# ScalarE copies a chunk's high part directly behind its square, on a three-stream block of Trainium2

## The chip, the core and the metric

The kernel runs on one core of one Trainium2 chip. The metric is device time in microseconds (us), smaller is better. Engines are named as in the profile: PE (TensorE), PEld (its weight loads), DVE (VectorE), ACT (ScalarE), POOL (GpSimd), SP (the queue that starts most transfers).

## What is computed

x is 32 sequences of 256 tokens of 128 numbers. The block is a "macaron": half a mixture of experts, attention, half a mixture of experts, each behind a layer norm.

```python
x = x + 0.5 * ffn(layernorm(x)); x = x + attention(layernorm(x)); x = x + 0.5 * ffn(layernorm(x))
# ffn: 8 experts, widths 4 x 128 and 4 x 256 (1536 columns in all), the best two of each token
topw, sel = top_k(sigmoid(xf @ router_w.T), 2); topw = topw / topw.sum(-1)
h = square(relu(einsum('td,edw->tew', xf, W1e)))
out = einsum('td,te->td', einsum('tew,ewd->ted', h, W2e), combine)
# attention: 16 heads of 8, rotary, linear: features elu + 1, k_feat^T v per sequence, then divided
```

## The kernel before, in words

Tokens go in 16 groups of 512. A group passes three streams: f1 (first expert layer), at (attention), f2 (second expert layer). One iteration t of a pipeline, written out on every engine, works on f1's group t+1, on attention's groups t-1 and t-2 and on f2's group t-4, and on the preparations of later groups. Iterations run from t = -3 to 21; f1 lives in t = -1 to 14, f2 in t = 4 to 19. From t = 4 to 13 both run at full density. Each engine's order is the order of the calls in its `iteration`; nothing but semaphores couples the engines.

Each expert layer is cut into NC = 12 chunks of 128 hidden columns. The functions of a chunk, in order:

- PE `up` (L532 to L534): three products, since a float32 product is made of a high and a low part of each operand, into one of two banks.
- DVE `weighted` (L1129): relu times the root of the expert's weight, into `hid`, a ring of six slots. Called "gate" below.
- ACT `squares`: the square L781, in place in `hid`, and the copy L792, which rounds to `h_hi`.
- POOL `remainders` (L942): `h_lo = hid - h_hi`; it frees the slot of `hid`.
- PE `down` (L555 to L557): three products with the second weights, nine places behind the chunk's `up`.

An iteration has 24 places, and three places make a quarter: PE's `quarter(t, j)` and ACT's `squares(t, j)` take quarter j. With both streams alive f1's chunks lie on places 0 to 11 and f2's on 12 to 23: three chunks a quarter. A stream that is alone (`alone`) has its chunks on every second place. `squares` waits for the gate before each square, for the square before its copy, and before the first copy of a quarter also for older `down` products, which free `h_hi`.

Around the quarters ACT does other work: `evacuate_x` copies transposed tokens from the bank `tp` to `xT` (L749), `copy_yT` (L808), `norm` (L736), `exp_logits` (L758, L762), `copy_attnT` (L834), and `rows_of_weights` (L770), which copies the transposed expert weights out of the same bank `tp` to `g_row`. PE's transposes into `tp` (L494) wait in `tp_free` for the last reader of the bank, L770 among them. Of ACT's order, quarters 0 and 1 end with L770 of f2; then come xT of the attention, yT, quarters 2 and 3, L834 and xT of f2 (which waits until POOL's L928 has made the attention's x_lo, since `xT` is one buffer).

DVE's `high_part` casts `xT` to `x_hi` (L1047); f2's stands behind place 12 of the gates, and behind it `spread_roots` (L1107, `pick`) of f1, then the gate of place 13. POOL's order has f1's `root_of_weights` (L934), the attention's `low_part` (L928) and so on between its remainders.

In `squares` the local `lag` is 1 where f2 has more groups to come, and 0 in the last iterations: with 1 a copy stands behind the square of the next chunk of its quarter.

Of the kernel before, what the change touches and what calls it, by code (L numbers as in the profile page):

```python
# [30 lines left out]
ACT = mybir.ActivationFunctionType  # L31
# [6 lines left out]
TG = BG * RT  # L38
# [8 lines left out]
NC = WTOT // P  # L47
CQ = NC // TG
STAGE = NC // 2
# [18 lines left out]
class Step:  # L68
# [14 lines left out]
    @property  # L83
    def last(self):
        return self.c + self.a * (self.trips - 1)

    @property
    def value(self):
        return self.i * self.a + self.c


def first(v):
    return v.c if isinstance(v, Step) else v
# [10 lines left out]
def due(v):  # L104

    assert (first(v) > 0) == (last(v) > 0)
    return first(v) > 0


def live(n):  # L110

    return first(n) >= 0 and last(n) < NG
# [7 lines left out]
def done(n):  # L120

    if last(n) <= 0:
        return 0
    if first(n) >= NG:
        return NG
    assert first(n) >= 0 and last(n) <= NG
    return n
# [41 lines left out]
def build(nc, x_in, wqkv, wout, router, w1, w2, const, out, rows):  # L169
    ctx = ExitStack()  # L170
    with ctx:
        def sb(name, shape, dt=F32):
            return ctx.enter_context(nc.sbuf_tensor(name, shape, dt))
# [20 lines left out]
        hid = sb("hid", [P, STAGE, NTOK])  # L194
        h_hi = sb("h_hi", [P, NC, NTOK], F32R)
# [88 lines left out]
        def per(name, keys):  # L284
            return {s: sem(f"s_{name}_{s}") for s in keys}
# [30 lines left out]
        s_z = per("z", FFN)  # L316
        s_sq = per("sq", FFN)
        s_hhi = per("hhi", FFN)
        s_hlo = per("hlo", FFN)
        s_p2 = per("p2", FFN)  # L320
# [7 lines left out]
        other = {"f1": "f2", "f2": "f1"}  # L328
        off = {"f1": 0, "f2": SHIFT}

        def turns(s, t):


            return done(t + 1 + (1 if s == "f2" else 0) - off[other[s]])

        def alone(s, t):


            return not live(t + 1 - SHIFT) if s == "f1" else not live(t + 2)
# [21 lines left out]
        def chunks(t, place, behind=0):  # L361


            out = []
            for s, start in (("f1", 0), ("f2", NC)):
                for back in range(2):
                    k = place + PLACES * back - start - behind
                    step = 2 if alone(s, t - back) else 1
                    n = t - back + 1 - off[s]
                    if live(n) and k % step == 0 and 0 <= k // step < NC:  # L370
                        out.append((s, n, k // step, back))
            return out
# [345 lines left out]
        def _(act):  # L718
            fn = nc.scalar.activation
# [52 lines left out]
            def squares(t, j):  # L772

                todo = [k for place in range(CQ * j, CQ * (j + 1)) for k in chunks(t, place)]
                lag = 0 if alone("f2", t if 2 * j >= TG else t - 1) else 1
                for k in range(len(todo) + lag):
                    if k < len(todo):
                        s, n, c, ago = todo[k]
                        h = hid[:, c % STAGE, :]
                        act.wait_ge(s_z[s], value(n * NC + c + 1))  # L780
                        fn(h, h, ACT.Square).then_inc(s_sq[s], 1)  # L781
                    if k >= lag:
                        s, n, c, ago = todo[k - lag]
                        if c % CQ == 0 or k == lag:
                            m = turns(s, t - ago) * TG + (c // CQ + 1 - TG)
                            if due(m):
                                act.wait_ge(s_p2[other[s]], value(m))
                            m = n * TG + (c // CQ + 1 - TG)
                            if due(m):
                                act.wait_ge(s_p2[s], value(m))  # L790
                        act.wait_ge(s_sq[s], value(n * NC + c + 1))
                        fn(h_hi[:, c, :], hid[:, c % STAGE, :], ACT.Copy).then_inc(s_hhi[s], 1)  # L792

            def copy_yT(s, n, t):
                if not live(n):
# [43 lines left out]
            def iteration(t, par):  # L839
                n1, n2, n2_last = t + 1, t + 1 - SHIFT, t - SHIFT  # L840
                evacuate_x("f1", t + 2, t, 0)
                squares(t - 1, 7)
                norm("at", t - 1)
                exp_logits("f1", t + 2)
                squares(t, 0)
                norm("f2", t + 2 - SHIFT)
                squares(t, 1)
                rows_of_weights("f2", n2)
                if alone("f1", t):
# [511 lines left out]
```

## Time and profile before

| | us |
|---|---|
| median of three runs | 774.03 |
| the three | 774.02, 774.03, 774.63 |
| the profiled execution | 772.65 |
| its span, first to last instruction | 770.8 |

The span is what the profile shows; 1.85 us of the profiled execution lie around it. TensorE's granted clock was 0.997 on average, that is its higher level throughout. Page rows give busy time, instruction count and, behind a bar, the idle time before a group of instructions with what ended most of it. Timeline rows give start, duration, engine, line, operation and tiles, a count where several were merged, and in brackets the idle time before with its releaser. Instructions of one engine overlap a little, so a start can lie before the end of the one before.

### The profile page before, as it was taken

The page shows a single profiled execution, that of the slowest core. Times are in us where ns is not written, and L with a number is a line of the kernel's source. Part 1 is how long each engine was busy: PE and PEld are TensorE (multiplying, and loading weights), DVE is VectorE, ACT ScalarE, POOL GpSimd, SP SyncE. Part 2 cuts the span into 40 slices and gives each one's busy share as a digit, 9 for nine tenths or more (in the row PEclk, how much of TensorE's full clock was granted, in tenths as well). Part 3 has the DMA queues.
Part 4 walks back from the last instruction along what each step waited for, and adds up shares of the span by engine and source line. Part 5 has one row for each costly group of instructions (what it writes and reads, how often), then busy time and mean ns, then how long its engine had stood idle before and what let it go on. Part 6 is the DMA issues. An engine that isn't in the chain of part 4 may idle for free.

```text
span 770.8 us, 13299 instructions
## 1 busy us (share of the span) xinstructions
PE 724.6 (94%) x3736; PEld 592.4 (77%) x3736; DVE 584.3 (76%) x1834; ACT 602.0 (78%) x1221; POOL 685.4 (89%) x663
## 2 busy tenths in 40 slices
PE   6899888789999999999999999999999999899888
PEld 6677676668888878888888888888887877777666
DVE  4767887887778797978778797978778587785554
ACT  4688767587888889788888889788878776767876
POOL 3899887879999999999999999999999877686986
PEclk9999999999999999999999999999999999999999
DMA  5553303212233332213333331323333302123331
GB/s 185 192 194 111 111 3 109 95 44 87 107 111 124 111 125 107 77 63 101 123 111 124 111 125 48 114 76 110 124 111 124 112 14 111 36 90 124 122 110 43
DMA packets 31176, 79.38 MB, mean 103 GB/s; under 512 B 3328, under 2 KB 14464, under 8 KB 31104
## 3 DMA queue, kind: packets, MB, share of 16 engines
q1 hardware_dynamic: 30816, 78.47, 29.9%
q8 instruction: 30, 0.49, 0.3%
q14 instruction: 42, 0.34, 0.1%
q10 hardware_dynamic: 288, 0.07, 0.1%
HBM read 73.81 MB, written 4.72 MB: 102 GB/s over the span
## 4 chain that ended last, share of the span: by engine, by line
PE 29%; DVE 27%; POOL 16%; issue 13%; ACT 11%; DMA 3%; DVEq 1%; POOLq 0%; ACTq 0%; SPq 0%
POOL h_lo L942 9%; DVE hid L1129 7%; PE bank L532 4%; PE bank L534 3%; PE bank L533 3%; PE bank L555 3%; POOL root_f L934 3%; PE bank L557 3%; PE bank L556 3%; ACT h_hi L792 3%; ACT hid L781 3%; DVE pick_f L1107 2%; DMA g_all_f<-rows_f 2%; PE bank L651 2%; PE bank L639 2%
## 5 line engine op out<-in xcount | busy, mean ns | idle before, releaser
L942 POOL TENSOR_TENSOR h_lo<-hid,h_hi 128x512 fp32r<-128x512 f32 x383 | 492.1, 1310 | 47.1 <-ACT h_hi L792 46.3
L1129 DVE SCALAR_TENSOR_TENSOR hid<-bank,g_all_f 128x512 f32<-128x512 f32 x384 | 262.6, 684 | 126.0 <-PE bank L534 87.9
L781 ACT ACTIVATE hid<-hid 128x512 f32<-128x512 f32 x384 | 229.6, 621 | 26.7 <-DVE hid L1129 26.1
L792 ACT ACTIVATE h_hi<-hid 128x512 fp32r<-128x512 f32 x384 | 229.0, 622 | 9.0 <-ACT hid L781 0.8
L532 PE MATMUL bank<-x_hi_f,w_hi 128*128 128x512 f32 x384 | 163.9, 427 | 13.5 <-DVE hid L1129 13.4
L555 PE MATMUL bank<-h_hi,w_hi 128*128 128x512 f32 x384 | 153.5, 400 | 4.7 <-POOL h_lo L942 4.5
L557 PE MATMUL bank<-h_hi,w_lo 128*128 128x512 f32 x384 | 152.1, 396 | 0.0
L534 PE MATMUL bank<-x_hi_f,w_lo 128*128 128x512 f32 x384 | 151.6, 395 | 0.0
L533 PE MATMUL bank<-x_lo_f,w_hi 128*128 128x512 f32 x384 | 151.5, 395 | 0.0
L556 PE MATMUL bank<-h_lo,w_hi 128*128 128x512 f32 x384 | 151.3, 394 | 0.0
L532 PEld LDWEIGHTS bank<-x_hi_f,w_hi 128*128 128x128 f32 x384 | 72.8, 190 | 37.4 <-DVE hid L1129 20.7
L555 PEld LDWEIGHTS bank<-h_hi,w_hi 128*128 128x128 f32 x384 | 72.2, 188 | 24.4 <-POOL h_lo L942 8.9
L534 PEld LDWEIGHTS bank<-x_hi_f,w_lo 128*128 128x128 f32 x384 | 72.5, 189 | 17.4
L557 PEld LDWEIGHTS bank<-h_hi,w_lo 128*128 128x128 f32 x384 | 72.2, 188 | 16.7
L556 PEld LDWEIGHTS bank<-h_lo,w_hi 128*128 128x128 f32 x384 | 72.2, 188 | 15.3
L533 PEld LDWEIGHTS bank<-x_lo_f,w_hi 128*128 128x128 f32 x384 | 73.1, 190 | 10.9
L934 POOL TENSOR_TENSOR root_f<-cwt_f,c_half 128x8 f32<-128x8 f32 x32 | 54.1, 1690 | 3.8 <-DVE cwt_f L1089 3.7
L736 ACT ACTIVATE xn_f<-x_sb,nbias_f,rstd_f 128x128 f32<-128x128 f32 x120 | 49.1, 481 | 8.0 <-POOL nbias_f L910 8.0
L928 POOL TENSOR_TENSOR x_lo_f<-xT,x_hi_f 128x512 fp32r<-128x512 f32 x32 | 41.5, 1298 | 11.3 <-DVE x_hi_f L1047 11.3
L749 ACT ACTIVATE xT<-bank 128x512 f32<-128x512 f32 x48 | 28.4, 592 | 27.8 <-PE bank L494 20.9
L758 ACT ACTIVATE ex_f<-bank 128x32 f32<-128x32 f32 x32 | 6.3, 198 | 43.4 <-PE bank L513 43.4
L1047 DVE CAST x_hi_f<-xT 128x512 fp32r<-128x512 f32 x32 | 20.6, 645 | 25.5 <-ACT xT L749 25.5
(118 smaller groups left out, 1050.4 us busy)
## 6 DMA issues: line engine op xcount, KB each, us to landing
g_all_f<-rows_f SPq DMA_DIRECT2D x128, 512.0 KB, 5.5
x_sb<-in_x SPq DMA_DIRECT2D x16, 256.0 KB, 3.4
out_x<-x_sb SPq DMA_DIRECT2D x15, 256.0 KB, 7.0
g_all_f<-in_w SPq DMA_DIRECT2D x2, 768.0 KB, 6.8
con<-in_const SPq DMA_DIRECT2D x1, 584.0 KB, 6.3
rows_f<-g_row_f SPq DMA_DIRECT2D x32, 16.0 KB, 1.4
out_x<-x_sb SPq DMA_DIRECT2D x2, 128.0 KB, 1.8
g_all_f<-in_wqkv SPq DMA_DIRECT2D x1, 192.0 KB, 6.5
```

The costliest lines, as they stand in the source:

```text
L532: mm(o, w1_hi[:, w], x_hi[s][u][:], start=True, stop=False)
L533: mm(o, w1_hi[:, w], x_lo[s][u][:], start=False, stop=False)
L534: mm(o, w1_lo[:, w], x_hi[s][u][:], start=False, stop=True).then_inc(s_p1[s], 1)
L555: mm(o, w2_hi[:, c, :], h_hi[:, c, :], start=(c == 0), stop=False)
L556: mm(o, w2_hi[:, c, :], h_lo[:, c, :], start=False, stop=False)
L557: i = mm(o, w2_lo[:, c, :], h_hi[:, c, :], start=False, stop=(c == NC - 1))
L736: i = fn(xn[s][:, k, :], tile, ACT.Identity, bias=shift[:, first + k:first + k + 1], scale=scale[:, first + k:first + k + 1])
L781: fn(h, h, ACT.Square).then_inc(s_sq[s], 1)
L792: fn(h_hi[:, c, :], hid[:, c % STAGE, :], ACT.Copy).then_inc(s_hhi[s], 1)
L934: gp.tensor_tensor(root[s][:], cwt[s][:], c_half[:], ALU.pow).then_inc(s_root[s], 1)
L942: gp.tensor_tensor(h_lo[:, c, :], hid[:, c % STAGE, :], h_hi[:, c, :].bitcast(F32), ALU.subtract).then_inc(s_hlo[s], 1)
L1129: v.scalar_tensor_tensor(hid[:, c % STAGE, :], hp[c % 2][:], 0.0, g_all[s][:, EXPERT[c], :], ALU.max, ALU.mult).then_inc(s_z[s], 1)
```

## The change

`squares` loses its `lag`. Every copy L792 now stands directly behind the square of its own chunk, in all iterations; waits and instructions are the same. Before, the order was such only from quarter 2 of t = 14 on.

```diff
                 todo = [k for place in range(CQ * j, CQ * (j + 1)) for k in chunks(t, place)]
-                lag = 0 if alone("f2", t if 2 * j >= TG else t - 1) else 1
-                for k in range(len(todo) + lag):
-                    if k < len(todo):
-                        s, n, c, ago = todo[k]
-                        h = hid[:, c % STAGE, :]
-                        act.wait_ge(s_z[s], value(n * NC + c + 1))
-                        fn(h, h, ACT.Square).then_inc(s_sq[s], 1)
-                    if k >= lag:
-                        s, n, c, ago = todo[k - lag]
-                        if c % CQ == 0 or k == lag:
...
+                for k, (s, n, c, ago) in enumerate(todo):
+                    h = hid[:, c % STAGE, :]
+                    act.wait_ge(s_z[s], value(n * NC + c + 1))
+                    fn(h, h, ACT.Square).then_inc(s_sq[s], 1)
+                    if c % CQ == 0 or k == 0:
+                        m = turns(s, t - ago) * TG + (c // CQ + 1 - TG)
+                        if due(m):
+                            act.wait_ge(s_p2[other[s]], value(m))
+                        m = n * TG + (c // CQ + 1 - TG)
+                        if due(m):
+                            act.wait_ge(s_p2[s], value(m))
+                    act.wait_ge(s_sq[s], value(n * NC + c + 1))
+                    fn(h_hi[:, c, :], hid[:, c % STAGE, :], ACT.Copy).then_inc(s_hhi[s], 1)
```

ACT's row in a two-stream iteration, from quarter 3 to the attention copy, f2's xT and f1's norm, before:

```order
L781 ACTIVATE hid<-hid 128x512 x2
L792 ACTIVATE h_hi<-hid 128x512
L781 ACTIVATE hid<-hid 128x512
L792 ACTIVATE h_hi<-hid 128x512 x2
L834 ACTIVATE attn<-bank 128x512
L749 ACTIVATE xT<-bank 128x512
L736 ACTIVATE xn_f<-x_sb,nbias_f,rstd_f 128x128 x4
```

and the same place now (the lines behind the function moved up by five, so L778 is the square, L787 the copy, L829 the attention copy):

```order
L778 ACTIVATE hid<-hid 128x512
L787 ACTIVATE h_hi<-hid 128x512
L778 ACTIVATE hid<-hid 128x512
L787 ACTIVATE h_hi<-hid 128x512
L778 ACTIVATE hid<-hid 128x512
L787 ACTIVATE h_hi<-hid 128x512
L829 ACTIVATE attn<-bank 128x512
L749 ACTIVATE xT<-bank 128x512
L736 ACTIVATE xn_f<-x_sb,nbias_f,rstd_f 128x128 x4
```

The first copy moved ahead of the second square and the second copy ahead of the third; what follows the quarter is in its old place.

ACT's row at quarter 1, with f2's norm ahead of it and the row of weights, xT of the attention and yT behind it, before:

```order
L736 ACTIVATE xn_f<-x_sb,nbias_f,rstd_f 128x128 x4
L781 ACTIVATE hid<-hid 128x512 x2
L792 ACTIVATE h_hi<-hid 128x512
L781 ACTIVATE hid<-hid 128x512
L792 ACTIVATE h_hi<-hid 128x512 x2
L770 ACTIVATE g_row_f<-bank,c_cut 32x128
L749 ACTIVATE xT<-bank 128x512
```

and now:

```order
L736 ACTIVATE xn_f<-x_sb,nbias_f,rstd_f 128x128 x4
L778 ACTIVATE hid<-hid 128x512
L787 ACTIVATE h_hi<-hid 128x512
L778 ACTIVATE hid<-hid 128x512
L787 ACTIVATE h_hi<-hid 128x512
L778 ACTIVATE hid<-hid 128x512
L787 ACTIVATE h_hi<-hid 128x512
L770 ACTIVATE g_row_f<-bank,c_cut 32x128
L749 ACTIVATE xT<-bank 128x512
```

The same exchange; L770 still stands behind the quarter's last copy. PE's, DVE's, POOL's and SP's orders are as before.

## Rows read from the trace of the kernel before

**Rows 1.** The page, busy time of each engine.
```profile
PE 724.6 (94%) x3736; PEld 592.4 (77%) x3736; DVE 584.3 (76%) x1834; ACT 602.0 (78%) x1221; POOL 685.4 (89%) x663
```

**Rows 2.** Busy time by stretch: stretch, its length, busy us of each engine, clock, DMA.
```profile
156.00:592.00 436.00, 430.35 (x2234) 358.24 (x2234) 351.94 (x1134) 361.12 (x754) 423.85 (x402) 1.00 0.31 103
...
300.00:343.57 43.57, 43.25 (x227) 36.11 (x226) 35.37 (x115) 36.42 (x76) 43.03 (x42) 1.00 0.31 104
```

**Rows 3.** The page, the costliest group of instructions.
```profile
L942 POOL TENSOR_TENSOR h_lo<-hid,h_hi 128x512 fp32r<-128x512 f32 x383 | 492.1, 1310 | 47.1 <-ACT h_hi L792 46.3
```

**Rows 4.** Timeline of ACT in the iteration from 300 us, quarters 2 and 3.
```profile
301.83 1.15 ACT L781 ACTIVATE hid<-hid 128x512 f32<-128x512 f32 x2
302.87 0.63 ACT L792 ACTIVATE h_hi<-hid 128x512 fp32r<-128x512 f32 x1
...
308.08 0.58 ACT L834 ACTIVATE attn<-bank 128x512 f32<-128x512 f32 x1
309.33 0.60 ACT L749 ACTIVATE xT<-bank 128x512 f32<-128x512 f32 x1 [0.67 <-POOL x_lo_at L928]
```

**Rows 5.** Timeline of POOL, the same place.
```profile
302.22 1.29 POOL L942 TENSOR_TENSOR h_lo<-hid,h_hi 128x512 fp32r<-128x512 f32 x1
...
303.58 1.30 POOL L942 TENSOR_TENSOR h_lo<-hid,h_hi 128x512 fp32r<-128x512 f32 x1
...
309.12 1.29 POOL L942 TENSOR_TENSOR h_lo<-hid,h_hi 128x512 fp32r<-128x512 f32 x1
...
310.38 1.46 POOL L942 TENSOR_TENSOR h_lo<-hid,h_hi 128x512 fp32r<-128x512 f32 x1
```

**Rows 6.** Timeline of DVE, the same iteration.
```profile
303.63 1.52 DVE L1047 CAST x_hi_at<-xT 128x512 fp32r<-128x512 f32 x1
...
309.96 0.73 DVE L1047 CAST x_hi_f<-xT 128x512 fp32r<-128x512 f32 x1 [2.11 <-ACT xT L749]
310.62 1.30 DVE L1107 TENSOR_TENSOR pick_f<-chosen_f,root_f 128x64 f32<-128x64 f32 x1
311.84 0.68 DVE L1129 SCALAR_TENSOR_TENSOR hid<-bank,g_all_f 128x512 f32<-128x512 f32 x1
...
330.91 0.41 DVE L1047 CAST x_hi_f<-xT 128x512 fp32r<-128x512 f32 x1
331.24 0.21 DVE L1107 TENSOR_TENSOR pick_f<-chosen_f,root_f 128x64 f32<-128x64 f32 x1
```

**Rows 7.** Timeline of ACT where the order is already the new one (t = 14).
```profile
605.86 0.63 ACT L781 ACTIVATE hid<-hid 128x512 f32<-128x512 f32 x1
606.60 0.63 ACT L792 ACTIVATE h_hi<-hid 128x512 fp32r<-128x512 f32 x1
607.14 0.62 ACT L781 ACTIVATE hid<-hid 128x512 f32<-128x512 f32 x1
607.79 0.63 ACT L792 ACTIVATE h_hi<-hid 128x512 fp32r<-128x512 f32 x1
...
609.51 0.61 ACT L781 ACTIVATE hid<-hid 128x512 f32<-128x512 f32 x1
610.52 0.63 ACT L792 ACTIVATE h_hi<-hid 128x512 fp32r<-128x512 f32 x1 [0.39 <-ACT hid L781]
```

**Rows 8.** Timeline, the row of weights on ACT and PE's transposes behind it.
```profile
342.82 0.34 ACT L770 ACTIVATE g_row_f<-bank,c_cut 32x128 f32<-32x128 f32 x1
...
343.79 0.60 PE L494 MATMUL bank<-con,xn_at 128*128 128x128 f32 x4
```

**Rows 9.** The lonely first stream: timelines of ACT and PE, and POOL's waits from 20 to 160 us.
```profile
66.70 0.62 ACT L781 ACTIVATE hid<-hid 128x512 f32<-128x512 f32 x1
...
68.75 1.14 ACT L792 ACTIVATE h_hi<-hid 128x512 fp32r<-128x512 f32 x2
...
137.33 1.16 PE L670 MATMUL bank<-wout_sb,attn 128*128 128x128 f32 x8 [0.23 <-ACT attn L834]
...
POOL h_lo L942 <- ACT h_hi L792: 12.0, 12, 1.9
```

More of the change, by code:

```diff
@@ L774, in squares @@
                 todo = [k for place in range(CQ * j, CQ * (j + 1)) for k in chunks(t, place)]
-                lag = 0 if alone("f2", t if 2 * j >= TG else t - 1) else 1
-                for k in range(len(todo) + lag):
-                    if k < len(todo):
-                        s, n, c, ago = todo[k]
-                        h = hid[:, c % STAGE, :]
-                        act.wait_ge(s_z[s], value(n * NC + c + 1))
-                        fn(h, h, ACT.Square).then_inc(s_sq[s], 1)
-                    if k >= lag:
-                        s, n, c, ago = todo[k - lag]
-                        if c % CQ == 0 or k == lag:
[L785 to L792, printed above, removed]
+                for k, (s, n, c, ago) in enumerate(todo):
[11 more added lines that the diff above has]
+                    fn(h_hi[:, c, :], hid[:, c % STAGE, :], ACT.Copy).then_inc(s_hhi[s], 1)
             def copy_yT(s, n, t):
```

## The prediction

> **What bounds the kernel now.** I read the profile from the outside in. The page first: a span of 770.8 us in which PE is busy 94%, GpSimd (POOL) 89% and ScalarE (ACT) 78% [rows 1]. That is an average over stages, so the table by stage comes next [rows 2]. From 156 to 592 us both mixture-of-experts streams run at full density: ten iterations, PE busy 430.35 of 436.00 us. The reader is to see one of them, from 300.00 to 343.57 us: PE busy 43.25 and POOL 43.03 of its 43.57 us, ACT 36.42. Two engines are full at once, so anything that makes either wait lengthens the iteration; ACT has room in the sum, but not at every place. Before 156 us the first stream is alone, and looser.
>
> POOL's bulk is 383 remainders of 1310 ns, one for each chunk, each behind one of ScalarE's copies L792 [rows 3]. Then the timelines, engine by engine, of that one iteration. On ACT, a quarter with three chunks issues its six instructions 0.52 us apart although each lasts 0.62; two quarters take 308.08 - 301.83 = 6.25 us [rows 4]. The first copy starts at 302.87 and ends at 303.50, and POOL's remainder starts at 303.58: POOL, whose remainder before ended at 303.51, waits for this copy by a hair [rows 5]. I call the start of this copy zero. From zero, POOL works without a pause; one of its operations ends and the next begins at +7.51 (310.38). On DVE, the cast L1047 of x_hi for the second stream is asked for at +7.09 (309.96, after 2.11 us of waiting for ACT's xT); pick L1107 follows, and the 14th gate of the iteration starts at +8.97 (311.84) [rows 6]. From there DVE's timeline shows no idle time until the attention's features, where it waits for ScalarE's exponential, and what it makes feeds PE, which is full until the transposes L494 that release ACT for the next zero. So there is a circle: zero, ACT's two quarters, attention copy, xT, cast, pick, DVE, PE, transposes, zero. It and POOL's own work are almost equally long, and both are 43.57.
>
> **The cost of the change, part by part.** No instruction is added or removed: 384 squares and 384 copies stay. The only order that moves is ACT's, in quarters of two or three chunks, up to the first two quarters of the iteration that begins at 592 us; from the third quarter of that one on the kernel has the new order already, and its rows there give the price.
>
> Part 1, the copy behind its own square. In the order already new (605.86 on) a quarter takes 609.51 - 605.86 = 3.65 us: square to copy 0.74 and then 0.65, copy to square 0.54 [rows 7]. The old quarter takes 6.25 / 2 = 3.12. So a three-chunk quarter costs ACT +0.53, and two neighbouring quarters +1.05. The first copy of a quarter, however, starts 0.74 behind its square and not 302.87 - 301.83 = 1.04: -0.30. One copy there started 1.01 behind its square (609.51 to 610.52); bound for that: nothing or +0.27 more in a quarter. I take nothing, since the others show 0.65 to 0.74.
>
> Part 2, zero comes 0.30 earlier for POOL and for everything counted from it: -0.30 an iteration on the circle.
>
> Part 3, the attention copy and xT behind two quarters. Today the attention copy starts at +5.21. New: 7.30 - 0.74 = +6.56. xT follows 0.48 behind (duration 0.58 less 0.10 of overlap) and takes 0.60, and DVE starts 0.03 behind its end: +7.67 instead of +7.09. Today's 0.67 us in which ACT waits there for POOL's x_lo [rows 4] swallows the rest. What is late next: the cast. The rows show what a DVE cast does beside a POOL remainder. L1047 lasts 0.41 us at 330.91, but 1.52 at 303.63, where it came 0.05 behind the start of a remainder, and it ended at 305.15, when that remainder had ended (304.88) [rows 5, 6]. pick lasts 0.21 at 331.24 and 1.30 at 310.62, ending at 311.92, just behind the end of a remainder at 311.84 (310.38 + 1.46). So these two run on DVE only between two POOL operations. Today the cast comes at +7.09, before the boundary at +7.51, and pick gets the boundary after that. At +7.67 the cast misses it by 0.16 us: it gets the next, one remainder later (310.38 - 309.12 = 1.26), and pick and the gate behind it move by as much: **+1.26 an iteration**. DVE and PE have no room behind it, so this reaches the next zero.
>
> The Trainium skill ("SBUF — State Buffer", Who interferes with whom) states that a VectorE operation in a 2-port mode, or with two SBUF inputs against a GpSimd operation that reads SBUF, blocks fully for the whole instruction, and casts and tensor_tensor are among them; the trace agrees [rows 5, 6]. By that rule the term is 1.26. If the long durations were no such lock and the cast merely came late, the term would be the delay itself, 0.58.
>
> Part 4, the row of weights. Two quarters before L770 make it 1.05 later: its end, 343.16 today, goes to 344.21. PE's transposes L494 (start 343.79) write the bank that L770 reads, and wait for it [rows 8]. The slack is 0.63 us, so at least 1.05 - 0.63 = +0.42; at most all 1.05, should PE's queue need after the release what it has today. DVE starts 0.03 behind the xT that it waits for [rows 4, 6], which speaks for the low end; with a little for PE's queue I take +0.60.
>
> An iteration: 1.26 + 0.60 - 0.30 = +1.56; ten of them, +15.6 us. POOL will then wait about 1.6 us for the copy at zero.
>
> Part 5, the lonely first stream (five iterations). Here a copy often waits for the next chunk's square, which waits for DVE: square 66.70, its copy 68.75 [rows 9]; new, 66.70 + 0.74 = 67.44, a gain of 1.3. All of POOL's waits for copies are 12.0 us, in 12 places, and only some lie on the path, in the first two iterations: I take -1.5 of bounds 0 and -2.6 (two of 1.3). In the later ones PE's output product waits for the attention copy [rows 9], which comes behind three chunks and so later by up to 0.53: for two such iterations +0.8. Together -0.7; if a window as in part 3 is missed there once, +0.6.
>
> **Sum:** +15.6 - 0.7 = +14.9 on a span of 770.8. The profiled run took 772.65, the median of three is 774.03; the difference is carried over unchanged: **788.9 us**. This case with its own bounds (part 4 from 0.42 to 1.05, part 5 from -2.6 to +1.4 around it) is 785 to 794.
>
> **The rivals.** (a) The window is kept: the cast still gets in before +7.51, since it misses by 0.16 us only and POOL's first operations could start later by as much. Then an iteration changes by 0.60 - 0.30 = +0.3: +3 - 0.7, 776.3. For it speaks the smallness of the miss; against it that POOL starts 0.08 behind the copy's end every time and that 0.05 was enough to lose at 303.63. (b) The delay is passed on with no lock: 0.58 + 0.3 = 0.88 an iteration, 782.1. Against it stand the picks of 1.30 us (one row shown for ten alike, [rows 6]). (c) Faster: the circle has hidden room (at the cast 2.11 us of idle DVE, at L494 0.63 of slack), POOL alone sets the period, and the copies that come early help. Then ten iterations give POOL's hair back, some 0.07 each (303.58 against 303.51), and the lonely stage up to 2.6: 771. It decides from there whether ACT's +1.05 in two quarters fits into its waits: it would if the 0.67 us before xT were 1.05. Against it: 0.67 is less. (d) Worse: L494 late by all of 1.05, the odd copy of 1.01 (+0.27) in each pair of quarters, and one more DVE operation meeting a remainder: 1.26 + 1.05 + 0.27 - 0.30 + about 0.4 = 2.7 an iteration, 800. (e) That the edit does nothing to the order is excluded: ACT's order shows the copies moved.
>
> **Chances.** Forecast 0.58, (a) 0.14, (b) 0.10, (c) 0.11, (d) 0.07. The range leaves out (c) and (d) for the most part: 775 to 794. About 0.2% is what a measurement of this kernel can tell from no change, 1.5 us. Faster by more than that: (c), 0.11. Within: the lower part of (a), 0.07. Slower: 0.82.
>
> **What would show it.** In the iterations between 156 and 592 us: period about 45.1 instead of 43.57; ACT's quarter of three 3.65; cast L1047 of the second stream over 1 us long and ending some 9.1 behind zero; the gate behind pick at about +10.2; L494 right behind L770; POOL idle 1.6 us before the remainder at zero, with PE's busy time unchanged in sum. A cast of 0.7 us or less there, or a POOL without idle time, would show part 3 wrong; L494 more than 0.5 us behind L770's end would show part 4 mis-sized. If the time is within 3 us of 774, the circle was not the bound.

## The result, and the profile after

| | before | after |
|---|---|---|
| median of the runs, us | 774.02 | 793.97 |
| lowest and highest | 773.54 to 774.63 | 792.7 to 794.29 |
| the profiled execution | 772.65 | 794.29 |
| its span | 770.8 | 792.5 |

The changed kernel is slower: ratio 1.0255, interval 1.024 to 1.0271. The forecast was 788.9 with a range of 775 to 794. The sign and the mechanism held; the size was 5.1 us too small, and the result stands at the very end of the range.

The page of the changed kernel, busy time of each engine, the chain that ended last by engine, and the groups of the remainder and of DVE's cast:

```profile
PE 731.4 (92%) x3736; PEld 593.0 (75%) x3736; DVE 597.6 (75%) x1834; ACT 629.9 (79%) x1221; POOL 683.6 (86%) x663
...
PE 38%; DVE 23%; ACT 19%; issue 12%; DMA 3%; POOL 3%; DVEq 1%; ACTq 0%; POOLq 0%; SPq 0%
...
L937 POOL TENSOR_TENSOR h_lo<-hid,h_hi 128x512 fp32r<-128x512 f32 x383 | 490.8, 1306 | 67.4 <-ACT h_hi L787 66.9
...
L1042 DVE CAST x_hi_f<-xT 128x512 fp32r<-128x512 f32 x32 | 28.0, 876 | 27.5 <-ACT xT L749 27.5
```

The same groups of before:

```profile
PE 29%; DVE 27%; POOL 16%; issue 13%; ACT 11%; DMA 3%; DVEq 1%; POOLq 0%; ACTq 0%; SPq 0%
...
L1047 DVE CAST x_hi_f<-xT 128x512 fp32r<-128x512 f32 x32 | 20.6, 645 | 25.5 <-ACT xT L749 25.5
```

POOL's remainders cost what they did (490.8 against 492.1 us, [rows 3]), but the time in which POOL waits for a copy rose from 47.1 to 67.4 us. POOL's own work fell from 16% to 3% of the chain that ended last; that share alone proves little, since pad_104 below, as fast as the kernel before, shows 3% as well. And a DVE cast, an instruction that nobody touched, became 231 ns longer on average.

**Where the time is.** Zero is, as in the prediction, the start of the first copy of quarter 2. Three zeros of after, with the square ahead of each, on ACT's timeline:

```profile
173.90 0.61 ACT L778 ACTIVATE hid<-hid 128x512 f32<-128x512 f32 x1
174.60 0.63 ACT L787 ACTIVATE h_hi<-hid 128x512 fp32r<-128x512 f32 x1
...
355.55 0.63 ACT L778 ACTIVATE hid<-hid 128x512 f32<-128x512 f32 x1
356.29 0.63 ACT L787 ACTIVATE h_hi<-hid 128x512 fp32r<-128x512 f32 x1
...
627.22 0.63 ACT L778 ACTIVATE hid<-hid 128x512 f32<-128x512 f32 x1
627.97 0.63 ACT L787 ACTIVATE h_hi<-hid 128x512 fp32r<-128x512 f32 x1
```

and the first of before, and two neighbouring ones (its last, at 606.60, stands in [rows 7]):

```profile
172.22 0.61 ACT L792 ACTIVATE h_hi<-hid 128x512 fp32r<-128x512 f32 x1
...
346.44 0.63 ACT L792 ACTIVATE h_hi<-hid 128x512 fp32r<-128x512 f32 x1
...
390.00 0.63 ACT L792 ACTIVATE h_hi<-hid 128x512 fp32r<-128x512 f32 x1
```

From the first to the last zero are ten periods: 453.37 us after, 434.38 before, so +18.99, that is +1.90 a period. Ahead of the first zero there is +2.38, behind the last 164.53 against 164.20, +0.33. Together 21.7 of 21.7 us of span. The ten iterations hold the loss. The medians differ by less than these two executions, 19.95 us; with 18.99 in the ten periods, some 1 us of them is left for all other stages.

**One period.** The period that begins at 356.29, DVE's timeline from the second stream's cast to the gate behind pick, then from cw_f on:

```profile
363.94 1.43 DVE L1042 CAST x_hi_f<-xT 128x512 fp32r<-128x512 f32 x1 [2.38 <-ACT xT L749]
365.30 1.30 DVE L1102 TENSOR_TENSOR pick_f<-chosen_f,root_f 128x64 f32<-128x64 f32 x1
366.52 0.68 DVE L1124 SCALAR_TENSOR_TENSOR hid<-bank,g_all_f 128x512 f32<-128x512 f32 x1
...
376.36 0.63 DVE L1080 TENSOR_TENSOR cw_f<-best_f,rtot_f 128x8 f32<-128x8 f32 x1
...
383.95 0.69 DVE L1202 SCALAR_TENSOR_TENSOR kf<-kb,ka 128x512 f32<-128x512 f32 x1 [0.79 <-ACT kb L813]
...
385.16 0.69 DVE L1124 SCALAR_TENSOR_TENSOR hid<-bank,g_all_f 128x512 f32<-128x512 f32 x1
385.76 0.47 DVE L1042 CAST x_hi_f<-xT 128x512 fp32r<-128x512 f32 x1
```

The cast now comes at +7.65, lasts 1.43 instead of 0.73 us [rows 6], and the gate behind pick starts at +10.23 instead of +8.97. It took the boundary that the prediction named: on POOL's timeline a block of three remainders begins at 362.55 (+6.26), so its second begins near +7.5 and its third near +8.8; the cast came behind the former and ended at 365.37, 0.3 us behind the latter.

```profile
357.00 1.31 POOL L937 TENSOR_TENSOR h_lo<-hid,h_hi 128x512 fp32r<-128x512 f32 x1 [1.81 <-ACT h_hi L787]
...
362.55 3.96 POOL L937 TENSOR_TENSOR h_lo<-hid,h_hi 128x512 fp32r<-128x512 f32 x3
```

cw_f, with two inputs in SBUF, is new in the story. In the same place of before it lasted 0.16 us, and kf lasted 0.91:

```profile
365.32 0.16 DVE L1085 TENSOR_TENSOR cw_f<-best_f,rtot_f 128x8 f32<-128x8 f32 x1
...
372.45 0.91 DVE L1207 SCALAR_TENSOR_TENSOR kf<-kb,ka 128x512 f32<-128x512 f32 x1 [0.80 <-ACT kb L818]
```

The end of the period, ACT's row of weights and PE's transposes behind it, up to the zero at 401.73:

```profile
398.80 0.34 ACT L770 ACTIVATE g_row_f<-bank,c_cut 32x128 f32<-32x128 f32 x1
...
399.35 0.63 PE L494 MATMUL bank<-con,xn_at 128*128 128x128 f32 x4 [0.54 <-issue]
...
401.73 0.63 ACT L787 ACTIVATE h_hi<-hid 128x512 fp32r<-128x512 f32 x1
```

The transposes start 0.21 us behind the end of L770 (399.14). Before there were 0.63 us between the two [rows 8].

For the whole sum I take the first stream's cast as a marker: before 330.91, which is 28.04 behind its zero [rows 4, 6]; after 385.76, +29.47. From the marker to L494: before 343.79 - 330.91 = 12.88 [rows 6, 8], after 13.59. From L494 to the next zero: before 346.44 - 343.79 = 2.65, after 2.38. So the period grew by 1.43 + 0.71 - 0.27 = 1.87 (45.44 against 43.57).

### The profile page after: what moved, and what is told of

Its sections match the earlier page's. It is cut to its first block, busy times and chain, and to the rows that moved or that the text cites. A ratio compares the mean times of both kernels' runs of the same rounds, so it can differ in the third digit from the quotient of the medians.

```text
span 792.5 us, 13299 instructions
## 1 busy us (share of the span) xinstructions
PE 731.4 (92%) x3736; PEld 593.0 (75%) x3736; DVE 597.6 (75%) x1834; ACT 629.9 (79%) x1221; POOL 683.6 (86%) x663
## 4 chain that ended last, share of the span: by engine, by line
PE 38%; DVE 23%; ACT 19%; issue 12%; DMA 3%; POOL 3%; DVEq 1%; ACTq 0%; POOLq 0%; SPq 0%
ACT h_hi L787 7%; ACT hid L778 6%; DVE hid L1124 6%; PE bank L532 5%; PE bank L534 5%; PE bank L533 5%; PE bank L555 5%; PE bank L557 4%; PE bank L556 4%; DMA g_all_f<-rows_f 2%; PE bank L651 2%; PE bank L639 2%; PE bank L513 2%; DVE pick_f L1102 2%; ACT kb L813 1%
## 5 line engine op out<-in xcount | busy, mean ns | idle before, releaser
L937 POOL TENSOR_TENSOR h_lo<-hid,h_hi 128x512 fp32r<-128x512 f32 x383 | 490.8, 1306 | 67.4 <-ACT h_hi L787 66.9
L787 ACT ACTIVATE h_hi<-hid 128x512 fp32r<-128x512 f32 x384 | 242.9, 633 | 26.1 <-ACT hid L778 1.5
L778 ACT ACTIVATE hid<-hid 128x512 f32<-128x512 f32 x384 | 237.4, 618 | 22.8 <-DVE hid L1124 22.4
L555 PEld LDWEIGHTS bank<-h_hi,w_hi 128*128 128x128 f32 x384 | 72.6, 189 | 21.7 <-POOL h_lo L937 6.0
L556 PEld LDWEIGHTS bank<-h_lo,w_hi 128*128 128x128 f32 x384 | 72.5, 189 | 15.6
L1042 DVE CAST x_hi_f<-xT 128x512 fp32r<-128x512 f32 x32 | 28.0, 876 | 27.5 <-ACT xT L749 27.5
L513 PEld LDWEIGHTS bank<-router_sb,xT 128*128 128x128 f32 x256 | 33.1, 196 | 3.0 <-ACT xT L749 1.6
```

What stands on the lines that cost most here:

```text
L555: mm(o, w2_hi[:, c, :], h_hi[:, c, :], start=(c == 0), stop=False)
L556: mm(o, w2_hi[:, c, :], h_lo[:, c, :], start=False, stop=False)
L937: gp.tensor_tensor(h_lo[:, c, :], hid[:, c % STAGE, :], h_hi[:, c, :].bitcast(F32), ALU.subtract).then_inc(s_hlo[s], 1)
```

## The experiments

The theory is that of the prediction: the two-quarter delay makes the cast miss a boundary of POOL's work (part 3), the row of weights holds back L494 (part 4), and nothing else matters. Rivals: the delay is passed on as it is, without a lock; the 2.4 us ahead of the first zero are the lonely stage's price; the period would be set by something else. All ratios are against the kernel before, run on the same chip in the same session (its medians there were 774.0 to 774.6), with a 95% interval in brackets. Positions in the table are relative to zero, read from the timelines, for the period that begins nearest to 350 us; the length of the cast in us stands in brackets.

| kernel | cast asked at (length) | gate behind pick | marker | marker to L494 | L494 to zero | period |
|---|---|---|---|---|---|---|
| before | +7.10 (0.74) | +8.98 | +28.04 | 12.88 | 2.65 | 43.57 |
| after | +7.65 (1.43) | +10.22 | +29.47 | 13.59 | 2.38 | 45.44 |
| q23_old | +7.09 (0.74) | +8.98 | +28.02 | 13.48 | 2.68 | 44.18 |
| q01_old | +7.65 (1.42) | +10.21 | +29.47 | 12.88 | 2.35 | 44.70 |
| q03_old | +7.10 (0.74) | +8.98 | +28.04 | 12.87 | 2.65 | 43.56 |
| pad_104 | +7.35 (0.47) | +8.98 | +28.04 | 12.88 | 2.65 | 43.57 |
| pad_135 | +7.65 (1.42) | +10.20 | +29.42 | 12.87 | 2.65 | 44.94 |
| xT_first | +7.15 (0.70) | +8.99 | +29.20 | 13.59 | 2.38 | 45.17 |
| gate_first | +7.64 (1.43) | gate first | +29.48 | 13.59 | 2.38 | 45.45 |
| gate_cw | +7.64 (1.42) | gate first | +29.15 | 13.59 | 2.39 | 45.13 |

### Parts of the change alone: q23_old, q01_old, q03_old

Each is the kernel before with one condition in `squares`. q23_old keeps the old order in quarters 2 and 3 of the ten full iterations:

```diff
-                lag = 0 if alone("f2", t if 2 * j >= TG else t - 1) else 1
+                lag = 1 if 4 <= t <= 13 and j in (2, 3) else 0
```

> The changed kernel, but in the ten iterations with both streams (t = 4 to 13) quarters 2 and 3 keep the old order; nothing else is undone. Window theory: the cast L1047 of the second stream comes again at +7.1 behind the first copy of quarter 2, lasts 0.7, the gate behind pick is back at +9.0, and a period falls from 45.46 to about 44.2 (less 1.25; the 0.27 that the first copy gains goes too, and the late row of weights, +0.72, stays). Total about 794.0 - 9.8 = 784. Rival, plain lateness without a lock (0.57 an iteration): about 791. Rival, ACT as a whole too full: half of the loss back, 784 as well, but then the cast would not jump from 1.4 to 0.7 us.

Measured: 780.82 us, ratio 1.0088 (1.0063 to 1.0114). The period is 44.18, the cast and the gate are where they were before, and what grew is marker to L494, by exactly the 0.60 of part 4. The time is 3 us under the expected 784, which had counted the old order in quarters 2 and 3 as worth 1.25 - 0.27 a period; it is worth 1.26 (45.44 - 44.18), because the 0.18 between gate and marker and 0.11 at L494 go with it. On q23_old's timelines the marker, ACT's row of weights, PE's transposes and the next zero:

```profile
381.02 0.41 DVE L1047 CAST x_hi_f<-xT 128x512 fp32r<-128x512 f32 x1
...
393.95 0.34 ACT L770 ACTIVATE g_row_f<-bank,c_cut 32x128 f32<-32x128 f32 x1
...
394.50 0.63 PE L494 MATMUL bank<-con,xn_at 128*128 128x128 f32 x4 [0.44 <-issue]
...
397.18 0.63 ACT L792 ACTIVATE h_hi<-hid 128x512 fp32r<-128x512 f32 x1
```

L770 ends 13.27 behind the marker, 1.02 later than before (343.16 - 330.91 = 12.25); the slack of 0.63 swallows part of that, and 0.21 for the release are added: 1.02 - 0.63 + 0.21 = 0.60.

q01_old is the mirror image, old order in quarters 0 and 1:

```diff
-                lag = 0 if alone("f2", t if 2 * j >= TG else t - 1) else 1
+                lag = 1 if 4 <= t <= 14 and j in (0, 1) else 0
```

> The changed kernel, but in the two-stream iterations quarters 0 and 1 keep the old order. Theory: the row of weights L770 is in time again, PE's transposes L494 are not held, a period is 45.46 - 0.72 = 44.7 and the total about 794.0 - 7 = 787. The cast still misses its window (1.4 us, gate at +10.2). If the late row of weights cost nothing, the total stays at 794.

Measured: 785.39 us, ratio 1.0162 (1.0133 to 1.0191); period 44.70. Marker to L494 is that of before, the cast has missed its boundary, and L494 to zero is 0.30 shorter, which is part 2. So +1.43 - 0.30 = +1.13. The two halves give 0.61 + 1.13 = 1.74 of the 1.87; the rest is in marker to L494, 13.59 with both against 13.48.

q03_old has the old order in quarters 0 to 3 and the new one in all others:

```diff
-                lag = 0 if alone("f2", t if 2 * j >= TG else t - 1) else 1
+                lag = 1 if 4 <= t <= 14 and j in (0, 1) or 4 <= t <= 13 and j in (2, 3) else 0
```

> Quarters 0 to 3 of the two-stream iterations in the old order, quarters 4 to 7 and everything else in the new. Theory: both causes are gone, period 43.6 to 43.8 (the 0.19 us between the gate behind pick and the last gate may stay, since quarters 4 to 7 are behind it), total 776.5 to 778.5 with the 2.4 us that the lonely stage lost. If the cost came from ACT's load in sum, half of 19 us would stay: 784.

Measured: 773.16 us, ratio 0.9994 (0.9976 to 1.0012), under the expected 776.5 to 778.5: neither 0.19 a period nor 2.4 us of the lonely stage stayed. Four of eight quarters take the new order for nothing: the whole price hangs on the four in front of L834 and of L770.

### The cliff alone: pad_104 and pad_135

The kernel before, ACT's order untouched, with spare copies ahead of the attention copy in the ten full iterations. They read the constants and write a buffer that nobody reads. pad_104 has the first two, pad_135 also the third, with 256 columns:

```diff
+                if 4 <= t <= 13:
+                    fn(pads[0][:, 0:512], con[:, 0:512], ACT.Copy)
+                    fn(pads[1][:, 0:512], con[:, 0:512], ACT.Copy)
+                    fn(pads[2][:, 0:256], con[:, 0:256], ACT.Copy)
```

> The kernel before, order untouched, with two spare copies of 128x512 on ACT ahead of the attention copy in the ten two-stream iterations; their output is used by nobody. They make the attention copy 1.04 us later. Window theory: xT waited 0.67 us anyway, so the cast comes at +7.36, before the boundary at +7.51: the window is kept, gate at +9.0, total 774 to 776. Plain lateness: the cast comes 0.27 us later, and the circle with it: 776.7. Load theory (ACT's extra work is what costs, as much as in the change): over 780.

> As pad_104, with a third spare copy of 128x256, 0.31 us more: the attention copy is 1.35 late, the cast comes at +7.67, behind the boundary. Window theory: the cast lasts 1.4 us, the gate stands at +10.2, a period is 44.8 and the total 774 + 12.5 = 786.5, a jump of about 12 us for 0.31 us of work. Plain lateness: 0.58 an iteration, 780, only 3 above pad_104.

Measured: pad_104 774.5 us, ratio 0.9997 (0.9973 to 1.0021); pad_135 787.29 us, ratio 1.017 (1.0136 to 1.0205). DVE's timeline of pad_104 (zero at 348.03):

```profile
355.38 0.47 DVE L1051 CAST x_hi_f<-xT 128x512 fp32r<-128x512 f32 x1 [2.37 <-ACT xT L750]
355.77 1.30 DVE L1111 TENSOR_TENSOR pick_f<-chosen_f,root_f 128x64 f32<-128x64 f32 x1
357.00 0.68 DVE L1133 SCALAR_TENSOR_TENSOR hid<-bank,g_all_f 128x512 f32<-128x512 f32 x1
```

and of pad_135 (zero at 351.74):

```profile
359.39 1.42 DVE L1052 CAST x_hi_f<-xT 128x512 fp32r<-128x512 f32 x1 [2.67 <-ACT xT L750]
360.73 1.29 DVE L1112 TENSOR_TENSOR pick_f<-chosen_f,root_f 128x64 f32<-128x64 f32 x1
361.94 0.68 DVE L1134 SCALAR_TENSOR_TENSOR hid<-bank,g_all_f 128x512 f32<-128x512 f32 x1
```

The first 1.04 us of added ScalarE work an iteration cost nothing that the times show: the cast comes 0.25 later, lasts 0.27 less and ends at the same place. That is as much ScalarE work as the change adds in two quarters, so ScalarE's load as such is not the price. The next 0.31 us cost 12.8 us in all, 1.4 a period. That is a step, not a slope, and rival (b), the delay passed on, falls with it: pad_104 would have cost its 0.25 a period, 2.5 us.

The first of pad_104's ten periods shows the same step inside one run. There POOL's boundary lay earlier, at +7.30 (zero at 172.39), and the cast, asked for at +7.33, had just missed it; DVE's cast and POOL's remainder:

```profile
179.72 1.54 DVE L1051 CAST x_hi_f<-xT 128x512 fp32r<-128x512 f32 x1 [2.92 <-ACT xT L750]
...
179.69 1.30 POOL L946 TENSOR_TENSOR h_lo<-hid,h_hi 128x512 fp32r<-128x512 f32 x1
```

That period took 44.76 us against 43.30 for the first of the kernel before. The nine others took what they did before.

### The lonely stage: lone_new and late_new

lone_new is the kernel before with the new order for t < 4, late_new the changed kernel with the old order for t < 4 (its condition is `lag = 1 if t < 4 else 0`).

```diff
-                lag = 0 if alone("f2", t if 2 * j >= TG else t - 1) else 1
+                lag = 0 if t < 4 or alone("f2", t if 2 * j >= TG else t - 1) else 1
```

> The kernel before with the new order in the lonely iterations of the first stream alone (t up to 3). Theory: the loss of 2.4 us before the first two-stream iteration comes from here alone: 776.4. The prediction's view of the stage: 773.3 (less 0.7).

> The changed kernel with the order of before in the lonely stage (t < 4), the new order from t = 4 on. All agree that the period between two zeros is 45.45 us, as in the changed kernel. If the 2.4 us by which the changed kernel's profiled execution came later to the first full iteration were caused by the order there, this run is 2 us faster than the changed kernel: 791.5. If the new order in the lonely stage is worth about 2 us, as the run with the new order there alone says (-0.25%), this run is slower than the changed kernel, 795 to 796. If neither, 794.

Measured: lone_new 771.47 us, ratio 0.9975 (0.9956 to 0.9994), while late_new took 793.62, ratio 1.0236 (1.0211 to 1.026), not different from the 793.97 of the changed kernel. The first says that the new order gains there, the second that it does nothing; neither says that it costs 2.4 us. before_gate and lone_gate (below) differ by this order alone and took 773.42 and 773.37, which again says nothing. The first zero in the profiled executions came at 170.7 to 173.6 in the five kernels with the old order in that stage, and at 170.1 to 176.5 in the nine with the new one, q23_old the latest and q01_old the earliest of all, although the two have the same program up to t = 4. So the +2.38 is of the size of what one execution differs from another, and the lonely stage's share stays open, between -2 and +2 us.

What such a difference consists of can be read in the changed kernel. DVE's sum of the keys (two inputs in SBUF) in the lonely stage:

```profile
119.18 1.66 DVE L1197 SCALAR_TENSOR_TENSOR ka<-ka,kb 128x512 f32<-128x512 f32 x1
...
123.43 1.51 DVE L1042 CAST x_hi_f<-xT 128x512 fp32r<-128x512 f32 x1
```

The same sum took 0.69 us in the profile of before. It met a remainder there, as the cast did in the full iterations.

### Can the window be bought back: xT_first and gate_first

If a missed boundary is most of the price, other orders should return it. xT_first is the changed kernel with xT of the second stream ahead of the attention copy on ACT:

```diff
-                copy_attnT(t - 2)
...
+                copy_attnT(t - 2)
```

> The changed kernel with one pair of ACT's calls exchanged: xT of the second stream ahead of the attention copy. Window theory: xT starts at +6.55 and the cast at +7.2, before the boundary at +7.51; the cast lasts 0.7, the gate is back at +9.0, the period 44.2, total 794.0 - 12.5 = 781.5, with the new order untouched. If PE's output product then waits for the later attention copy, some of it comes back. Rival (the two quarters' added time costs wherever it lies): 792 to 794.

Measured: 793.48 us, ratio 1.0237 (1.0208 to 1.0266). The expectation missed by 12 us, though its mechanism came true: the cast got its boundary again (+7.15, 0.70 long) and the gate behind pick was back at +8.99. But PE did not move with zero. Against zero its output product L670 starts at +7.76, where it was +7.48 in the kernel before, because zero, the copy close behind its square, is itself some 0.3 earlier. It is not the later attention copy that holds it: in the changed kernel, where that copy is 0.47 earlier, L670 starts at +7.77, and in both PE has no idle time before it (in xT_first its weight load waited 0.18 us for the copy, without moving the product). With the cast in time, PE is what comes last: DVE waits 0.24 us for it ahead of the gate at +11.24 (+10.95 before), so 0.28 a period is lost there, and at +22.18 DVE's comparison for the experts misses a boundary (+21.93). PE's product in xT_first and in the changed kernel, then DVE's timeline of xT_first, cast and gate, and this comparison:

```profile
361.06 1.06 PE L670 MATMUL bank<-wout_sb,attn 128*128 128x128 f32 x8
...
364.07 1.05 PE L670 MATMUL bank<-wout_sb,attn 128*128 128x128 f32 x8
```


```profile
360.46 0.70 DVE L1042 CAST x_hi_f<-xT 128x512 fp32r<-128x512 f32 x1 [1.90 <-ACT xT L749]
...
362.30 0.68 DVE L1124 SCALAR_TENSOR_TENSOR hid<-bank,g_all_f 128x512 f32<-128x512 f32 x1
...
375.49 1.12 DVE L1092 TENSOR_TENSOR chosen_f<-which_f,con 128x64 f32<-128x64 uint32 x1
```

It lasted 1.12 instead of 0.19 us. The marker came at +29.20, only 0.27 earlier than in the changed kernel. Even that does not show in the total: the ten periods took 450.55 us, 2.8 less, but what lies behind the last zero took 169.1 instead of 164.5. The exchange stands in all iterations, and 2.8 us of it are there in the stage of the second stream alone (a copy 87.1 us behind the last zero in the changed kernel comes at 89.9 here); no run tests the exchange there by itself.

gate_first is the changed kernel with the gate of place 13 ahead of cast and pick on DVE, where DVE is idle:

```diff
+                weighted(t, 13)
                 high_part("f2", n2, p2)
                 spread_roots("f1", n1, 0)
-                weighted(t, 13)
```

> The changed kernel with DVE's gate of place 13 ahead of the cast and pick, so that PE does not wait for a gate behind them. Window theory: the cast still misses the window and lasts 1.4 us, but the gates of places 14 and on are what is late now; PE has one chunk more before it waits, about 1.4 us of work, so most of the 1.25 us an iteration is hidden: 783 to 788. If the cost were elsewhere: 794.

Measured: 793.79 us, ratio 1.0253 (1.0226 to 1.028), a miss too. Gate 13 started at +5.97 instead of +10.22, and up to +19.6 all that DVE does came 0.44 earlier than in the changed kernel. There the gain ends, in one instruction:

```profile
373.70 0.69 DVE L1163 TENSOR_TENSOR bank<-bank,con 128x512 f32<-128x512 f32 x1
374.30 1.07 DVE L1080 TENSOR_TENSOR cw_f<-best_f,rtot_f 128x8 f32<-128x8 f32 x1
375.29 0.68 DVE L1124 SCALAR_TENSOR_TENSOR hid<-bank,g_all_f 128x512 f32<-128x512 f32 x1
```

cw_f came 0.44 earlier and lasted 0.44 longer (1.07 against 0.63), for 8 elements in each partition. It ended at 375.37. On POOL's timeline three remainders fill 3.82 us from 374.05 on, so the first ends near 375.3:

```profile
374.05 3.82 POOL L937 TENSOR_TENSOR h_lo<-hid,h_hi 128x512 fp32r<-128x512 f32 x3
```

### The same with cw_f moved: gate_cw

From the two misses came a theory: an operation with two inputs in SBUF waits for the next boundary of POOL's work, so a gain ahead of it reaches only as far as it. That is to be tested by moving cw_f. gate_cw is gate_first with one more exchange:

```diff
+                weigh_two("f2", n2, 0)
                 rope_q_cos(t - 1)
-                weigh_two("f2", n2, 0)
```

> The changed kernel with gate 13 ahead of cast and pick (that alone: 793.8, caught again at cw_f, which then lasted 1.07 us), and cw_f moved ahead of rope_q_cos, so that it is asked for at about +19.0, just before a boundary of POOL's work (+19.37). Theory of the repeated catching: cw_f 0.5 us or less, gate 20 at about +20.1 instead of +20.6, the 0.5 us are kept up to +25, and are swallowed in part where ka meets a remainder at +26; the first gate behind the attention's features at +28.3 to +28.9 instead of +28.88; time 788 to 794. Rival (the period is set by something else than DVE's stream, the position of cw_f is idle detail): the gate behind the features at +28.88 with idle DVE time ahead of it, 794.

Measured: 790.23 us, ratio 1.0196 (1.0175 to 1.0218). DVE's timeline of gate_cw (zero at 356.60):

```profile
375.63 0.16 DVE L1080 TENSOR_TENSOR cw_f<-best_f,rtot_f 128x8 f32<-128x8 f32 x1
375.71 0.69 DVE L1163 TENSOR_TENSOR bank<-bank,con 128x512 f32<-128x512 f32 x1
376.31 0.68 DVE L1124 SCALAR_TENSOR_TENSOR hid<-bank,g_all_f 128x512 f32<-128x512 f32 x1
...
379.24 0.62 DVE L1092 TENSOR_TENSOR chosen_f<-which_f,con 128x64 f32<-128x64 uint32 x1
...
382.31 0.86 DVE L1197 SCALAR_TENSOR_TENSOR ka<-ka,kb 128x512 f32<-128x512 f32 x1
...
385.16 0.69 DVE L1124 SCALAR_TENSOR_TENSOR hid<-bank,g_all_f 128x512 f32<-128x512 f32 x1
```

cw_f lasted 0.16, the gate behind it started at +19.71 instead of +20.6, and the next two operations with two SBUF inputs took back 0.43 (0.62 against 0.19) and 0.17 (0.86 against 0.69). What was left at the gate behind the features is 0.32 a period: +28.56 instead of +28.87, ten times that is 3.2 us, and the time fell by 3.6 against gate_first. In the profiled executions the ten periods took 450.13 us against 453.40 in gate_first. So the theory held, although its range was wide (788 to 794); the rival, that cw_f's place does not matter, would have left 794.

### The gate ahead of the cast without the change: before_gate and lone_gate

before_gate is gate_first's exchange on the kernel before, lone_gate the same with the new order for t < 4, as tries for something faster than both.

> The kernel before with the gate of place 13 ahead of the second stream's cast and pick, so that DVE fills part of the 2.1 us in which it waits for xT. DVE's gate 13 at about +5.97, gate 14 at about +9.1 instead of +9.7. Theory (the DVE stream is caught again at its next operation with two SBUF inputs, and POOL alone needs 43.5): period 43.56 and 774. Rival (the circle through DVE is the longer one, POOL's 43.03 busy us the floor): up to 0.5 us an iteration, 769.

> The same, with the new order of squares and copies for t < 4: a try for a kernel faster than both. Theory: 771 to 772 (the -0.25% of the lonely stage alone, nothing from the gate). Rival: 767.

Measured: 773.42 us, ratio 0.9992 (0.9975 to 1.0009), and 773.37, ratio 0.9984 (0.9968 to 1.0). The period of before_gate is 43.54. Its gate 14 started 0.44 earlier, and the gain ended at the very next gate, which waits for PE:

```profile
354.75 0.68 DVE L1137 TENSOR_TENSOR x_sb<-bank,x_sb 128x512 f32<-128x512 f32 x1
355.83 0.69 DVE L1129 SCALAR_TENSOR_TENSOR hid<-bank,g_all_f 128x512 f32<-128x512 f32 x1 [0.40 <-PE bank L534]
```

That gate starts at +10.95, as in the kernel before (357.39 - 346.44). So here it was not, as I had expected, an operation in SBUF that swallowed the gain, but PE. lone_gate missed its expected 771 to 772: it took what before_gate took. No kernel of the study is faster than the kernel before by more than 0.25%.

## Why the prediction was right, point by point

**The size.** Forecast were +14.9 us, measured are +19.95. Of the 5.1 us, 3.4 lie in the ten periods (18.99 against 15.6) and the rest outside them (some +1 by the medians, where the forecast had -0.7). That 793.97 lies inside the range at all is luck: its upper end is 794, one of the four executions took 794.29, and the range was not what its own bounds give. Part 4 at 1.05 makes 2.01 a period, +20.1, and part 5 at +1.4 makes 795.5 at the top, not 794.

**Part 1** held. Three copies behind their squares take ACT 359.20 - 355.55 = 3.65 us, and the attention copy starts at 362.84, +6.55, where the prediction had +6.56. The copy at 1.01 us distance appeared once in the ten periods (its square at 512.87).

**Part 2** held: L494 to zero is shorter by 0.27 to 0.30 (after, q01_old). Only "everything counted from it" was too much: PE does not move with zero, which costs nothing as long as DVE behind the cast is later, and cost xT_first its 0.28.

**Part 3** held in mechanism and size. Cast at +7.65 (forecast +7.67), gate at +10.23 (forecast +10.2), +1.25 against +1.26. pad_104 and pad_135 show the cause by itself, with ACT's order of squares untouched. The Trainium skill ("SBUF — State Buffer", Who interferes with whom) was cited for the full block, and the alternative beside it, 0.58 for a cast that merely comes late, fell: the trace agrees with the page.

**Part 4** held alone and was mis-sized together with part 3: q23_old shows +0.60, the changed kernel 0.71. There L770 itself starts 13.04 behind the marker instead of 12.93; why, no run shows.

**What was missing** is the term between the gate behind pick and the marker, +0.18 a period (1.43 - 1.25). The prediction said that DVE has no room behind the gate and that the delay reaches the next zero. It put nothing for a change of the other operations on the way, and they do change: cw_f cost 0.47 more (0.63 against 0.16) and kf 0.22 less (0.69 against 0.91), both have two inputs in SBUF, and the whole stream stood elsewhere against POOL's boundaries; the 0.07 left over lie between the gate and cw_f (9.84 against 9.91). With the 0.11 at L494 and 0.03 less in part 2 that gives the 0.3 by which 1.56 fell short of 1.87; over ten periods 18.99 against 15.6. Behind the marker a third one changed, the first stream's pick: 1.31 us at +29.86, where it was 0.21 before [rows 6]. That cost nothing: it lasts as long in q01_old, whose marker to L494 is 12.88 as before, since DVE stands idle ahead of later gates anyway (0.90 and 0.95 us in the kernel before).

**Part 5** had -0.7 where the profiled execution had +2.38 ahead of the first zero. lone_new (-0.25%) takes the forecast's side, late_new and lone_gate (no change) take neither; the prediction put both signs into its bounds, and the sign stays open.

**POOL's wait** ahead of the remainder at zero was forecast at 1.6 us and is 1.81 (the row at 357.00 above).

**The rivals.** (a), the window kept, came true only where the cast came 0.25 later (pad_104) or 0.05 (xT_first), not at 0.55. (b) fell with the pads. (c) fell with the result, since ACT's added time did not fit into its waits; and where copies or gates came earlier at no cost (q03_old, before_gate), nothing was gained either, though in before_gate it was PE and not POOL that took the gain. (d) named one more DVE operation meeting a remainder, at 0.4 a period; that much was right in kind, and its net size was 0.18.

## What to carry to other kernels

Where two engines run at the same beat and one of them may start some operations only between two operations of the other, work added on a third engine costs nothing until it crosses a boundary, and then one whole operation: read from the timelines how far each such operation stands ahead of its boundary, and treat a miss of 0.15 us as a miss. A delay or a gain is then not carried along: it can grow or shrink at every later operation of that kind, so look up the next two or three of them before summing, and whether the engine has idle time behind them, which makes even a long one free. When an order gives such a boundary back, look at once for the path that comes last then; here it was PE. Of an instruction order that looks neutral ("the same work, one place earlier"), test the places apart: here four of eight quarters were free, two cost 0.6 a period and two 1.1.

## What the runs showed of the hardware

- A 128x512 cast on DVE asked for at +7.10 lasted 0.74, at +7.35 0.47, at +7.65 1.42: its end was fixed by POOL (+7.83, +7.82, +9.07), not its length. Where a remainder had begun only 0.03 us before it, it lasted 1.54 (pad_104, at 179.72).
- An operation of 8 elements a partition (cw_f) took 0.16, 0.63 or 1.07 us, depending on where it met POOL's remainder; one of 64 (chosen_f) 0.19, 0.62 or 1.12.
- A copy on ACT behind the square that it depends on starts 0.65 to 0.75 us after it (once in the ten periods 1.01), against 0.52 for one that depends on an older square: two quarters cost ACT 7.30 instead of 6.25 us, with the same twelve instructions.
